# Layer 1 features of a graph-attention kernel: three of eight heads' normalisation moved from VectorE to GpSimd

## The reference, cut to what matters

```python
z = jax.ops.segment_sum(ex, dst, num_segments=n)
alpha = ex / (z[dst] + 1e-16)
msg = h[src] * alpha[:, :, None]
out = jax.ops.segment_sum(msg, dst, num_segments=n)
out = out.reshape(n, heads * out_c) + bias      # layer 0, concat
h = jax.nn.elu(out)
h2 = h @ W2                                     # layer 1
al_s = einsum('nhc,hc->nh', h2, a_src2); al_d = einsum('nhc,hc->nh', h2, a_dst2)
```

## Time and profile before

| what | us |
|---|---|
| median of 3 runs | 2342.52 |
| lowest and highest | 2341.03, 2344.23 |
| the profiled execution's own time | 2348.46 |
| its span in the trace | 2346.7 |
| PE busy (76% of the span) | 1781.8 |
| VectorE busy (56%) | 1313.8 |
| GpSimd busy (55%) | 1280.8 |
| ScalarE busy (29%) | 687.7 |

### The profile page before, as it was taken

The page is one execution under the profiler, slowest core; times in us unless marked ns, Lnnn a source line. Parts: engine busy times, 40 slices in busy tenths (PEclk is TensorE's granted clock), DMA queues, the critical chain, the costliest instruction groups (busy, mean ns, idle before and its releaser), DMA issues. The chain is left out here.

```text
span 2346.7 us, 32245 instructions
## 1 busy us (share of the span) xinstructions
PE 1781.8 (76%) x8803; PEld 964.8 (41%) x8804; DVE 1313.8 (56%) x2948; ACT 687.7 (29%) x1707; POOL 1280.8 (55%) x1295
## 2 busy tenths in 40 slices
PE   1878877967777777575778967777777597899997
PEld 1346544522222222153444522223322276677775
DVE  6767776478888888594774024444444527122221
ACT  1611111311110111172222344544444261233332
POOL 5057774067777777321410257777777400577775
PEclk9989988999999999898999989998899886899998
DMA  5434321289999999895784989999999786588886
GB/s 183 128 81 107 73 55 30 96 282 338 340 339 338 339 339 338 301 262 150 197 245 104 246 295 355 353 353 357 357 355 354 255 283 253 112 140 137 135 142 99
DMA packets 178211, 542.44 MB, mean 231 GB/s; under 512 B 39169, under 2 KB 69612, under 8 KB 177874
## 3 DMA queue, kind: packets, MB, share of 16 engines
q0 software_dynamic: 99600, 379.31, 54.4%
q1 hardware_dynamic: 60242, 122.30, 15.3%
q10 hardware_dynamic: 18288, 39.93, 4.4%
HBM read 454.31 MB, written 87.12 MB: 231 GB/s over the span
## 5 line engine op out<-in xcount | busy, mean ns | idle before, releaser
L1694 PE MATMUL acc<-ring,work 128*64 128x384 f32 x880 | 183.2, 540 | 78.3 <-DMA ring<-feat_tab,src_t 39.6
L1476 PE MATMUL acc<-ring,work 128*64 128x388 f32 x880 | 182.8, 542 | 72.7 <-DVE ring L1453 58.5
L909 PE MATMUL acc<-wg,work 128*128 128x384 f32 x600 | 221.3, 516 | 7.3 <-ACT work L969 7.2
L1228 PE MATMUL acc<-wg,work 128*128 128x384 f32 x600 | 211.0, 500 | 18.7 <-ACT work L1285 18.7
L2128 POOL DMA_INDIRECT out_rows<-ring,wg x114 | 178.0, 1561 | 80.5 <-ACT ring L2225 58.2
L1603 POOL DMA_INDIRECT ring<-feat_tab,src_t x196 | 185.5, 947 | 59.7 <-issue 41.7
L1423 POOL DMA_INDIRECT ring<-feat_tab,src_t x196 | 185.3, 946 | 59.7 <-issue 44.4
L1453 DVE TENSOR_TENSOR ring<-ring,mps 128x776 f32<-128x776 f32 x196 | 185.1, 961 | 48.8 <-DMA ring<-feat_tab,src_t 46.8
L1772 ACT ACTIVATE work<-big,edges 128x64 f32<-128x64 f32 x392 | 135.9, 427 | 246.6 <-PE acc L1694 246.6
L859 POOL DMA_INDIRECT edges<-score_tab,src_p x168 | 166.3, 990 | 54.1 <-issue 52.8
L1662 DVE COPY work<-acc 64x384 f32<-64x384 f32 x100 | 56.0, 560 | 247.7 <-PE acc L1694 246.0
(11 more groups left out here) (383 smaller groups left out, 3457.1 us busy)
## 6 DMA issues: line engine op xcount, KB each, us to landing
ring<-lo_rows SPq DMA_DIRECT2D x49, 256.0 KB, 6.2
edges<-in_w_slow SPq DMA_DIRECT2D x28, 384.0 KB, 6.9
edges<-in_w_hebb POOLq DMA_DIRECT2D x28, 384.0 KB, 7.2
edges<-in_w_fast POOLq DMA_DIRECT2D x28, 384.0 KB, 8.4
unit_sum<-edges SPq DMA_DIRECT2D x28, 384.0 KB, 6.3
out_rows<-ring ACTq DMA_DIRECT2D x52, 192.0 KB, 4.5
feat_tab<-work ACTq DMA_DIRECT2D x25, 388.0 KB, 2.6
agg_raw<-work ACTq DMA_DIRECT2D x25, 388.0 KB, 5.5
```

What stands on the lines that cost most here:

```text
L909: m = nc.tensor.matmul(acc[:, sl * 2 + c, 0:C // 2], xT[sl][:, k, :], wg[:, k, c * (C // 2):(c + 1) * (C // 2)], start=(k == 0), stop=(k = ...
L1228: m = nc.tensor.matmul(acc[:, sl * 2 + c, 0:C // 2], xT[sl][:, k, :], wg[:, k, c * (C // 2):(c + 1) * (C // 2)], start=(k == 0), stop=(k = ...
L1476: m = nc.tensor.matmul(acc[c * WIN:(c + 1) * WIN, bank, 0:HALF], hot, row[:, c * HALF:(c + 1) * HALF], start=start, stop=True, skip_group_ ...
L1694: m = nc.tensor.matmul(acc[c * WIN:(c + 1) * WIN, bank, 0:n], hot, row[:, c * CHUNK:c * CHUNK + n], start=start, stop=True, skip_group_che ...
```

## The change

On line 656 two semaphores are added, `z_ready` (VectorE to GpSimd) and `y_pool` (GpSimd to PE and SP). VectorE makes the first five heads, GpSimd the last three, in two instructions over 288 columns: the product with the reciprocals, and the sum with the bias. PE's transposes and SP's row loads wait for both. GpSimd's unit loads were a loop of their own, and are now issued behind the work of a block: step j after block j + 7.

```diff
+            chain_p = sem("pool" + L)
+            on_pool = 3
...
                     for b in range(RB, NB):
                         sp.wait_ge(y_ready, b - RB + 1)
+                        sp.wait_ge(y_pool, b - RB + 1)
                         load(b)
...
                 @block.gpsimd
                 def _(pool):
-                    for j in range(EARLY + 1):
+                    st = Steps(pool, chain_p)
+
+                    def unit_step(j):
                         if j < EARLY:
                             pool.wait_ge(scaled, j + 1)
                             pool.dma_start(unit[j], part("w_hebb", j), accum_op=ALU.add).then_inc(unit_hebb[j], 16)
                         if j > 0:
                             pool.wait_ge(unit_hebb[j - 1], 16)
                             pool.dma_start(unit[j - 1], part("w_fast", j - 1), accum_op=ALU.add).then_inc(unit_fast[j - 1], 16)
+                    pool.wait_ge(b_in, 16)
+                    for b in range(NB):
+                        row = rows[b % RB].rearrange("p (h c) -> p h c", h=H)
+                        pool.wait_ge(z_ready, b + 1)
+                        if b >= 3:
+                            pool.wait_ge(yT_ps, b - 2)
+                        own = slice((H - on_pool) * (C // H), C)
+                        st.step(nc.gpsimd.tensor_tensor(y[b % 3][:, own].rearrange("p (h c) -> p h c", h=on_pool), row[:, H - on_pool:H, 0:HC - 1],
+                                                        row[:, H - on_pool:H, HC - 1:HC].to_broadcast([P, on_pool, HC - 1]), ALU.mult))
+                        nc.gpsimd.tensor_tensor(y[b % 3][:, own], y[b % 3][:, own], bias[:, own], ALU.add).then_inc(y_pool, 1)
+                        if 0 <= b - 7 <= EARLY:
+                            unit_step(b - 7)
...
                         st.step(V.reciprocal(z, z))
+                        dve.sem_inc(z_ready, 1)
                         if b >= 3:
                             dve.wait_ge(yT_ps, b - 2)
-                        for h in range(H):
+                        for h in range(H - on_pool):
...
                     def transposes(b):
                         pe.wait_ge(y_ready, b + 1)
+                        pe.wait_ge(y_pool, b + 1)
```

More of the change, by code:

```diff
@@ L655, in features_next @@
             places = [mps[0:2, j, 0:P] for j in range(2)]
-            scale_in, scaled = sem("scale_in" + L), sem("scaled" + L)
+            scale_in, scaled, z_ready, y_pool = (sem(n + L) for n in ("scale_in", "scaled", "z_ready", "y_pool"))
+            chain_p = sem("pool" + L)
+            on_pool = 3
             unit_in, unit_hebb, unit_fast = ([sem(f"{n}{h}" + L) for h in range(EARLY)] for n in ("unit_in", "unit_hebb", "unit_fast"))
```

## The result

| | median us | runs | lowest, highest |
|---|---|---|---|
| before | 2343.38 | 4 | 2341.03, 2345.80 |
| changed | 2368.02 | 4 | 2364.46, 2369.72 |

The ratio is 1.0097, with a 95% interval of 1.0082 to 1.0111: the change costs 24.6 us (19 to 26). I had forecast slower, but by 12 us; the time lies inside my range, near the upper end, where rival A was (2361 to 2367).

The account below looks back on a forecast made before the run. VectorE, DMA and the unit-load chain were taken as nearly level. Holding by the chain, +8.6 us, and engine disturbance, +3, summed to about +12 us: 2354.5 us on the median of 2342.52, range 2344 to 2370.

Parts of the forecast that it names:

- rival A: Exclusion: VectorE's quotients stand still while GpSimd reads, in every free block, period 3.96 us; +18 to +25 us; chance 0.28.
- B: Unit loads on GpSimd's queue speed up as rows and stores spread; at 4.0 us a step, 2338.7 us; gain's chance 0.08.
- C: Full saving: hebb always landed, nothing held, 0.69 us a block saved, up to 17 us, 2325; chance 0.02.
- step 2: GpSimd's two new elementwise instructions of 128x288 take 0.75 us each, 1.5 us a block (0.66 to 1.96).
- Step 5: VectorE and GpSimd disturb each other in blocks 19 to 24: 0.5 us a block, 3 us; bounds nothing to 9 us.
- step 1: VectorE loses three of eight quotients, 0.69 us a block, 17 us over 25 blocks if unlimited; semaphore increment taken as 0.
- Step 4: Called decisive: unit loads on GpSimd's queue hold blocks 8 to 16 at 5.8 us each; store of scores 8.6 us later.

Follow-up runs that it names:

- e1: Changed kernel without GpSimd's product and sum: VectorE makes all eight heads, GpSimd only passes the block on and issues unit loads; 2358.43 against 2344.08 us, ratio 1.0056.
- e10: Changed kernel with GpSimd starting a block only when VectorE's five quotients are done, increment of z_ready gone, unit steps still between blocks; ratio 1.0055, part +14.9 us.
- e2: Changed kernel with unit steps behind every second block and unit-sum stores behind the last row load, GpSimd's work kept; 2355.55 us, ratio 1.0044.
- e11: Kernel before run again unaltered for a second profile; one run, part 93.90 us against 93.35 in the first.
- e3: Changed kernel with GpSimd's product and sum turned into memsets of the same 288 columns, writing but reading nothing; ratio 1.0055, part +11.9 us.
- e8: Changed kernel with GpSimd starting after the quotients, stores last, unit steps behind every second block, fast two steps behind its hebb; ratio 0.9989, part -4.4 us.
- e9: Kernel e8 with unit steps one block later, behind blocks 7, 9, ... 23, the last behind 24; ratio 0.9965, part -6.2 us against the kernel before.
- e4: Kernel before with VectorE's quotients for five heads only and nobody making the other three; ratio 0.9987, part -2.7 us.
- e5: Changed kernel without the increment of z_ready, GpSimd waiting on VectorE's own step semaphore instead; ratio 1.0077, part 113.81 us.
- e12: Changed kernel run again unaltered; ratio 1.0079 to the kernel before, part 113.96 us.

## Why the prediction was right and wrong

**Right.** The direction, and the step that I called decisive. GpSimd waits for a hebb landing in seven of the eight steps, seven steps from fast 0 to fast 7 take 39.25 us (40.43 before), so the held products stand 5.6 us apart in the mean (5.4 to 5.8 in the last three steps, 3.2 to 7.0 before), and nine blocks are left at the last fast. Holding alone costs 15.1 us in e1 and 14.9 in e10, exclusion alone 7.6 in e2; their sum, 22.5 to 22.7, is near the 20.7 of the whole. Rivals B and C are out. GpSimd's instructions cost what step 2 had: 0.67 and 0.91 us, 1.6 for my 1.5. The estimate by the Trainium skill, 0.62 us apiece ("GPSIMD Engine Reference", "Elementwise — side-by-side cycle accounting"), is 0.05 us short for the product; the sum, with a second full input, takes 0.17 to 0.29 us more.

**Wrong: the size, in two terms of the sum.**

*Step 5, exclusion.* I took 0.5 us a block for the last six, since "the product may wait at no cost to VectorE". The product does not wait: it starts in the same moment as the quotients (1077.52 and 1077.53), and VectorE loses 1.0 us, plus 0.1 for the increment that step 1 had at 0. Six blocks at 3.56 for 2.46 us are 6.6 us, not 3: **3.6 us of the miss**. This was rival A with 1.1 us a block in place of its 1.5. It should have been the forecast. The rule of the Trainium skill that I cited ("SBUF — State Buffer", "Who interferes with whom") fits what the runs show in three ways: the quotients, with two SBUF inputs, are held up by GpSimd instructions that read; not by memsets (e3); and the ELU, with one of its inputs in PSUM, is not held up (e8). I gave it 0.28 because no row showed it, although it named the very operands.

*Step 4, where the chain begins.* I set fast 7 at 1 us earlier than before; from the first addition it came 78.65 us in, for 74.13 before and 73.1 forecast: **5.5 us**. By then exclusion had cost as well: blocks 3 to 7 at 3.57 us put hebb 0 2.75 us later than before (0.4 us in e10, whose free blocks take 2.65 us). Then hebb 0 landed, and fast 0 followed, 8.2 us behind its issue and not 5.3:

```profile
1012.61 0.99 POOL L702 DMA_DIRECT2D edges<-in_w_hebb  x1
...
1020.82 0.87 POOL L705 DMA_DIRECT2D edges<-in_w_fast  x1 [3.73 <-DMA edges<-in_w_hebb]
```

In the other runs with this chain it was 6.1 to 8.8 us, 6.1 in the kernel before itself when it ran again (e11), and what sets it was not separated. The seven steps then took 1.2 us less than before: 2.75 + 2.95 - 1.2, and the 1 us earlier that I had forecast, are the 5.5. That 1 us was there to be had: in e3, with blocks of 2.57 us, hebb 0 is issued 27.2 us behind the first addition, for 28.4 before and 31.2 in the changed kernel. So some 3.75 of the 5.5 us go with the slower free blocks, and the rest, 1.75 us of landing, is open. I had counted exclusion only in blocks 19 to 24, and forgotten that free blocks at the start set when the chain can begin.

*What step 4 left to the range.* e10 has free blocks of 2.65 us and is still 14.9 us longer, of which 0.8 lies before fast 7. Behind fast 7 it takes 33.3 us, 14.1 more than before; the steps of the prediction with 2.65 us give 10.8 more. PE's half clock fits 1.9 us of the rest: in e10 the two pieces of block 16, the first behind fast 7, take 1.51 + 2.72 us for 0.87 + 1.47.

```profile
1223.43 1.51 PE L762 MATMUL acc<-ident,work 128*128 128x128 f32 x6 [3.58 <-issue]
1224.87 2.72 PE L771 MATMUL mps<-big,wa 128*2 128x128 f32 x12
```

From the start of block 24 to the store it is 12.1 us there against 10.97, another 1.1; from PE's transposes of that block on it is 8.5 us in both, so this lies in GpSimd's late start. In the changed kernel itself what follows fast 7 takes 35.4 us against my 28.8 + 3: the 3.6 us of exclusion cover that difference. That the slower blocks hide PE's delay there is my reading; the second ELU behind fast 7 waits 1.57 us for its exponential in e10, 1.46 in e3 and 0.74 in e1, and not at all in the changed kernel.

Together 5.5 + 3.6 us on 11.6 give the 20.7 of the part. That the time is still inside my range is owed to the width that rival A had given it; the later chain was in none of its bounds. **Open** stays the further 3.9 us between the part's 20.7 and the median's 24.6: the repeat has 20.1 and 22.5, and the part's 20.7 lies inside the interval of 19 to 26, so there may be nothing to explain. I did not try to raise PE's clock during the holding, nor to run quotients with the bias in PSUM: its only spare columns share banks with PE's transposes.

## What to carry to other kernels

A queue that carries both a DMA chain with its waits and work that others wait for makes every block as slow as the chain: put the wait where the landing is past, two steps behind and on every second block in e8 and e9, or keep the queue for one of them. Moving elementwise work from VectorE to GpSimd paid here only when the two did not run beside each other with VectorE reading two SBUF operands (e8, e9 against e2): start GpSimd's share behind those, beside an instruction with a PSUM operand. And take away the cost alone first (e4): it showed that even a free saving would have given 2 to 3 us, because the row loads stood behind stores that waited.

## What the runs showed of the hardware that I had not expected

- A GpSimd instruction that reads SBUF and a two-input VectorE one that start together cost VectorE most of GpSimd's time (1.0 us for 1.6), and GpSimd little: product 0.67 us beside the quotients and the same 0.67 beside the ELU (e8); the sum goes from 0.79 to 0.91.
- The quotients are held one at a time and to the end: in the free block shown, the first ends 0.1 us behind the product and the third 0.1 us behind the sum, and the other three take 0.30 us each.
- Two GpSimd memsets of the same shape in the same place cost VectorE nothing in its quotients (0.25 us apiece).
- An increment of a semaphore between two VectorE instructions takes 0.11 us of a full queue (3.26 for 3.15 us a block), and half of that or less where the next instruction is held up anyway.
- VectorE's small addition (128x8, strided, one input) is held as well, although it has one SBUF input: in the changed kernel it took 0.17 us, or up to 1.28. In the six traces with three heads on GpSimd in which it was held by a product or sum (changed, e5, e8, e9, e10, e12) it took over 0.2 us 41 times, and each time it ended 0.03 to 0.04 us behind the end of one; started 0.04 us ahead of the sum it took 0.17. In 12 of the 41 it had started before the product's record, during the issue of the fast load ahead of it. A DMA issue alone held it in a few blocks (0.33 us in e2, 0.53 in e3) and not in most; that was not settled.
- A product directly behind a DMA issue on GpSimd's own queue is shown with 0.98 us and not 0.67; its record starts 0.3 us before the record of the issue ends (1054.83 against 1054.26 + 0.86).
